# Weighted values in eight equal pieces, with a fourth buffer of values

## The reference

```python
q, k, v = heads(x @ Wq + bq), heads(ctx @ Wk + bk), heads(ctx @ Wv + bv)   # 16 heads of 8
scores = einsum('bhqd,bhkd->bhqk', q, k) / sqrt(8)
scores = scores - m * 1e6                     # attention 3 only
out = softmax(scores) @ v                     # 1500 keys for each of 56 queries
y = merge(out) @ Wo + bo                      # attention 1 has no biases
```

## Time and profile before

| | us |
|---|---|
| median of three executions | 7436.17 |
| the profiled execution | 7445.05 |
| its span, first to last instruction | 7443.3 |
| attention 1, first `shifted` to last | 2417.9 to 3495.6 |
| attention 3, first `shifted` to last | 6199.6 to 7310.5 |
| busy over the span: PE, DVE, ACT, POOL | 6207.6, 5417.4, 3220.7, 2008.9 |

### The profile page before, as it was taken

The page is one execution under the profiler, slowest core; times in us unless marked ns, Lnnn a source line. Parts: engine busy times, 40 slices in busy tenths (PEclk is TensorE's granted clock), DMA queues, the critical chain, the costliest instruction groups (busy, mean ns, idle before and its releaser), DMA issues. The chain is left out here.

```text
span 7443.3 us, 114698 instructions
## 1 busy us (share of the span) xinstructions
PE 6207.6 (83%) x41440; PEld 3959.6 (53%) x41440; DVE 5417.4 (73%) x8622; ACT 3220.7 (43%) x5922; POOL 2008.9 (27%) x952
## 2 busy tenths in 40 slices
PE   4777777777776799998899869999999966888887
PEld 2444444444442677777544434444444444777776
DVE  7999999999983677777333367777777744777774
ACT  2444444444442455555222234444444423555552
POOL 2544445444440222221000001111111102333330
PEclk7999999999986899999999989999999977999998
DMA  2000000000101666664000010000000006878771
GB/s 65 28 29 25 25 29 27 28 27 25 29 10 41 122 131 135 126 134 75 24 24 15 8 29 17 17 15 14 17 17 17 4 10 130 148 150 145 142 148 19
DMA packets 238867, 412.99 MB, mean 55 GB/s; under 512 B 71028, under 2 KB 138465, under 8 KB 238353
## 3 DMA queue, kind: packets, MB, share of 16 engines
q1 hardware_dynamic: 238464, 407.82, 26.6%
HBM read 330.35 MB, written 77.40 MB: 55 GB/s over the span
## 5 line engine op out<-in xcount | busy, mean ns | idle before, releaser
L1356 DVE CUSTOM_DVE_ANT_0 attn_logits<-attn_scores,attn_shift 112x750 f32<-112x750 f32 x1024 | 942.9, 930 | 465.0 <-PE attn_scores L1173 464.2
L1276 ACT ACTIVATE attn_probs_t<-attn_pt 125x448 f32<-125x448 f32 x1536 | 831.3, 542 | 783.6 <-PE attn_pt L1188 763.1
L470 POOL TENSOR_TENSOR attn_shift<-attn_bias,attn_push 112x1500 f32<-112x1500 f32 x256 | 862.9, 3374 | 1102.9 <-DVE attn_top L924 1057.5
L594 PE MATMUL attn_scores<-attn_k_t,attn_q_blocks 128*112 128x500 f32 x1536 | 857.0, 654 | 188.0 <-DVE attn_v L791 111.6
L1188 PEld LDWEIGHTS attn_pt<-ident,attn_logits 112*125 112x125 f32 x6144 | 868.2, 191 | 223.2 <-issue 80.2
L1188 PE MATMUL attn_pt<-ident,attn_logits 112*125 112x112 f32 x6144 | 927.2, 274 | 69.1 <-DVE attn_logits L1370 43.0
L2046 PE MATMUL attn2k_pk<-attn_wk,attn2k_cn_t 128*125 128x512 f32 x1536 | 737.9, 602 | 39.4 <-ACT attn2k_cn_t L2117 36.6
L510 PEld LDWEIGHTS attn_pt<-ident,attn_probs 112*125 112x125 f32 x3072 | 450.6, 194 | 569.7 <-issue 269.1
L2057 PE MATMUL attn2k_pg<-attn2k_kn,attn2k_cn 125*128 125x512 f32 x1536 | 725.0, 594 | 4.5 <-ACT attn2k_gram L2125 2.3
L661 ACT ACTIVATE attn_probs<-attn_probs,attn_neg_top 112x1500 f32<-112x1500 f32 x256 | 395.5, 1545 | 697.2 <-DVE attn_neg_top L933 697.2
L2212 DVE TENSOR_REDUCE attn2k_ss<-attn2k_sq 125x16 f32<-125x1024 f32 x384 | 467.0, 1216 | 255.5 <-ACT attn2k_sq L2154 255.5
(11 more groups left out here) (280 smaller groups left out, 10327.4 us busy)
## 6 DMA issues: line engine op xcount, KB each, us to landing
attn_k_packed<-k_scratch SPq DMA_DIRECT2D x384, 375.0 KB, 5.7
attn_ctx_t<-in_ctx_t SPq DMA_DIRECT2D x96, 750.0 KB, 6.8
k_scratch<-attn_k_parts SPq DMA_DIRECT2D x64, 1125.0 KB, 7.1
attn2k_ctx<-in_ctx SPq DMA_DIRECT2D x32, 750.0 KB
attn_mask<-in_mask SPq DMA_DIRECT2D x64, 328.1 KB
attn_shift<-in_mask SPq DMA_DIRECT2D x64, 328.1 KB
attn_out_t<-in_mask_t SPq DMA_DIRECT2D x32, 328.1 KB
ffn_gu<-in_experts_up_t SPq DMA_DIRECT2D x8, 938.0 KB
```

The lines of the kernel that those rows point to most:

```text
L470: pool.tensor_tensor(shift[:, p % 2, :], bias[:, p, :], push[:], ALU.add).then_inc(shift_ready, 1)
L594: mm = pe.matmul(scores[bank(step, j)][0:PAIR, c, 0:THIRD], q_blocks[:, j, 2 * step:2 * step + 2, :].rearrange("p a s -> p (a s)"), (k_pac ...
L1276: act.activation(probs_t[0:KC, p // 4, 4 * t:4 * t + 4, (p % 4) * PAIR:(p % 4 + 1) * PAIR], pt[(3 * at + t) % 2][0:KC, 0:QUAD].rearrange(" ...
L1356: dve.tensor_tensor_reduce(out=logits[:, at % 3, cols].rearrange("p (b k) -> p b k", b=2), in0=scores[h][0:PAIR, :, 0:QTR], in1=shift[:, n ...
```

## The change

`v` gets a fourth buffer, and `v_columns` and `weigh` take it by `n % 4`; `hold_values` waits for a sequence one further back. `weigh` is called in every pair, with a quarter of a group (3 chunks, 12 matmuls): grp 0 of n in pairs 6 and 7 of n and in pairs 0 and 1 of n+1, grp 1 of n in pairs 2 to 5 of n+1. `mix(n-1)` moves on ACT from behind pair 4 to ahead of pair 6. At the end of the last sequence the second half of grp 0 and all of grp 1 follow the last turns.

```diff
-        v = r.sb("v", [KC, 3, CH, VROW])
+        v = r.sb("v", [KC, 4, CH, VROW])
...
-                        if p in (6, 7):
-                            weigh(n, 0, FIRST if p == 6 else SECOND)
-                        if p in (2, 3) and n > 0:
-                            weigh(n - 1, 1, FIRST if p == 2 else SECOND)
+                        if p > 5:
+                            weigh(n, 0, quarter(p - 6))
+                        elif n > 0:
+                            weigh(n - 1, 0 if p < 2 else 1, quarter(p + 2 if p < 2 else p - 2))
...
-                weigh(B - 1, 1, FIRST)
-                weigh(B - 1, 1, SECOND)
+                weigh(B - 1, 0, range(CH // 2, CH))
+                weigh(B - 1, 1, range(CH))
...
+                        if p == 6 and n > 0:
+                            mix(n - 1)
...
-                        if p == 4 and n > 0:
-                            mix(n - 1)
...
-                        wait(dve, pv_ready, 2 * (n - 2))
+                        wait(dve, pv_ready, 2 * (n - 3))
```

More of the change, by code:

```diff
@@ L1022, in v_columns @@
         def v_columns(n, b):
-            return v[:, n % 3, 4 * b:4 * b + 4, 0:HP * V1].rearrange("p c (h e) -> p c h e", e=V1)[:, :, :, 1:V1]
+            return v[:, n % 4, 4 * b:4 * b + 4, 0:HP * V1].rearrange("p c (h e) -> p c h e", e=V1)[:, :, :, 1:V1]
         with nc.Block() as block:
@@ L1201, in weigh @@
                             last = pe.matmul(po[32 * j:32 * j + 32, grp * PAIR:(grp + 1) * PAIR],
-                                             v[:, n % 3, c, V1 * p:V1 * p + 32],
+                                             v[:, n % 4, c, V1 * p:V1 * p + 32],
                                              probs_t[0:KC, grp, c, j * PAIR:(j + 1) * PAIR],
@@ L1214, in _, with quarter @@
                         values(n, i)
-                FIRST, SECOND = range(0, CH // 2), range(CH // 2, CH)
+                def quarter(i):
+                    return range(i * CH // 4, (i + 1) * CH // 4)
                 def side_work(n, p):
```

## The result

The changed kernel takes 7562.16 us (median of four executions, 7558.46 to 7568.04), the one before 7437.56 (median of four, 7434.36 to 7447.63). The ratio is 1.0166, with a 95% interval of 1.0148 to 1.0184: 124.6 us slower. The forecast was 7512, its range 7425 to 7562; the result is 0.2 above that range's top, and near the 7557 of rival 4.

What follows compares the result with a forecast made beforehand. PE and DVE take turns holding up the sequence, so the change was priced pair by pair: 7445.05 + 56 (pieces) + 20 (clock) = 7521 profiled; the median lies 8.9 lower, so 7512, range 7425 to 7562.

Steps and rivals of the forecast that it cites:

- rival 4: The clock falls in nearly every sequence of both attentions: +45 on the forecast, 7557; chance 0.12.
- The price of a piece and the seams: On PE, a quarter of `weigh` takes 0.71 us to the next score; a new piece's seam adds 0.10.
- rivals 1 and 3: 1: seams are free, 7406, with the clock 7426 (0.06). 3: PE's slack takes new pieces, only gains count, 7341 (0.07).
- rival 2: PE has cover in pairs 4 and 5 by a lead from earlier pairs: 7434, no change; chance 0.08.
- The push in attention 3: POOL's `push` stalls DVE's `lower`, so pair 3's gain is lost there; pair 5 pays +0.46 us.
- Pair 3 and the fourth buffer: The buffer removes `hold_values`' wait, 1.29 us each; PE's 4.42 us then sets pair 3 instead of 5.37: -0.95.
- The fill of v: Ahead of each attention, filling `v` grows from 4.63 to 6.17 us, twice; cost between 0 and 3.1 us, taken as 0.
- The clock: A wider PE gap ahead of `out` brings more, dearer clock falls: +20 us, bounds -43 and +55; the softest term.
- the 56 us: Cost of the pieces, summed over the pairs of both attentions: 1.93 us for each of 29 sequences.

Runs made afterwards that it cites:

- the two fills: Unused matmuls put into PE's gap ahead of `out`: four in the changed kernel, 7465.66 us; three in the kernel before, 7403.64 us.

## Why the prediction was right, and where it was not

**The price of a piece and the seams: right.** A quarter takes 0.72 us to the next score, forecast 0.71. All sixteen pairs of the table come out as worked: pair 0 3.63 (3.63), pairs 1 and 2 4.39 (4.39), pair 3 4.42 (4.42), pair 7 4.94 (5.51 - 0.58 = 4.93). Pairs 4 and 5 of attention 1 are 3.69 and 3.61, forecast 3.66 each: PE gets a lead of 0.05 there, no more. The sum was 1.03 and 0.90 a sequence, the table has 1.02 and 0.88. T(2) - T(1) of 4.39 excludes rivals 1 and 3, and T(6) - T(5) of 3.61 in attention 1 excludes rival 2. (Rival 2's sum was wrong too: 7512 - 58 is 7454; its 7434 leaves out the clock's 20.)

**The push in attention 3: right.** `lower` of pair 3 took 3.77 us (forecast near 3.8) and T(5) - T(3) stayed at 10.55; pair 5 has 2.88, +0.44 (forecast +0.46). `push` of the same sequence, in POOL's timeline of the changed kernel:

```profile
6598.83 4.00 POOL L1094 TENSOR_SCALAR attn_shift<-attn_shift 112x1500 f32<-112x1500 f32 x1
```

It ends at 6602.83 and `lower` at 6599.85 + 3.77 = 6603.62, 0.79 us behind it; before it was the same 0.79 with a start 0.9 us later against the push. With the push out of its way `lower` takes 1.00: the stall belongs to the overlap. The Trainium skill, "SBUF — State Buffer", Who interferes with whom, says that a `tensor_scalar` of DVE in a 2-port mode and a GpSimd instruction exclude each other for the whole instruction. These numbers agree in kind; the 0.79 is less than a whole `lower` of 1.00, which that rule alone does not give.

**Pair 3 and the fourth buffer: right.** No wait for `po` is left, and with the buffer alone pair 3 takes 5.00, PE's own, as the working had it.

**The fill of v: right.** It takes 6.14 us (forecast 6.17). From its start to the first `shifted` are 56.0 us in attention 1 for 57.8 before, and 65.5 in attention 3 for 65.8: it costs nothing. The 5.5 us outside the two attentions lie ahead of the first fill, which starts at 2367.63 for 2360.06, behind stages that the change leaves alone. The same start varies among the twelve profiles, with three buffers as with four: attention 1 begins between 2408 and 2424.

**The clock: the step that was mis-sized.** The prediction took +20 and bounded it by -43 and +55; it measured +63 by the table and +63 by the two fills. Its parts:
- The gap ahead of `out` is 1.99 us in every sequence of both attentions, forecast 1.8 to 2.0. That was right.
- I let attention 3 fall in two of five sequences; it falls in 18 of 29, up from 3. All 29 pay, 22 of them 0.4 to 1.0 us and seven 3.3 to 3.5, as a fall late in one sequence runs on into pair 0 of the next. Measured: +34.
- I priced a fall at 1.6, and it costs 2.2. The low stretch reaches on through pair 0, as in PE's timeline above, and pair 0 is now PE's too.
- Two of five sequences at 1.6 are already 19 of the 20 us, so the term left nothing for attention 1, where the prediction expected more and dearer falls. There are 28 there for 21. Measured: +29.

The upper bound was wrong for the same reason: it took one fall a sequence at the price of a short one. Rival 4 had the direction, more falls in attention 3. That its 7557 is only 5 below the result is partly luck: it wanted a fall in nearly all 58 sequences at 1.6 us, there are 46 at 2.2, and by the prediction's own +55 its sum is 7547 (7436 + 56 + 55).

So the direction and the 56 us were worked out soundly, and half of the loss was the term called the softest. The trace before had one long fall in these sequences: number 22 of attention 3 takes 36.38 us for 34.02, with the clock low from 7008.6 us on for 6.8 us. At that price 58 falls are 137 us, 98 above the 39 paid before, a bound that holds the result. The prediction followed one short stretch, and that to the end of its `weigh`.

## What to carry to other kernels

Price a split piece pair by pair, at the place where it will stand: behind the last thing that the next engine waits for it costs its full length and its seams, in front of a wait of its own engine nearly nothing (125 us over the kernel before and 79 under it, for the same eight pieces). On PE such a wait can be worth more than its length, as filling it can keep the clock up too: in attention 1 here it did, in attention 3, with its second wait, only in part. Before a change shortens work ahead of a wait, take the fall of the clock at its longest seen, followed to where the clock comes back, as the upper bound for every turn of the loop.

## What the hardware did that I had not expected

- The clock falls although PE is never idle for longer than some 2 us and is 87 to 90% busy in the windows. In attention 1, out of 29 sequences: a gap of 1.03 us ahead of `out` went with 2 falls, 1.21 with 21, 1.41 with 23, 1.59 with 29 and 1.99 with 28. Length alone does not decide: with 1.23 us and the pieces ahead of the side work attention 1 has 8 falls; with 1.21 us, attention 3 has 3 falls before and 23 once `push` is moved and its sequences are as short as those of attention 1; with 1.99 us it has 18. What decides is open. The Trainium skill, "TensorE: Matmul & The Clock Gate", HAM oscillation, tells of a fall where single waits of PE are long, in every tile of a loop; the repetition agrees in attention 1 (28 of 29), but the waits here are shorter than those of its example.
- Three or four useless matmuls in that gap are worth 39 us in the kernel before and 102 in the changed one.
- PE can stand for 4.7 us with nothing that the profile shows to wait for, in a stretch where the DMA engines are full. Its cause is open.
